# Two softmax attentions: scores from 32 bit operands in four row groups instead of three-part bf16 operands

## The reference, cut to what matters

```python
# layer 1, attn: causal self attention, 16 heads of 16 features
q, k = rope(x @ wq), rope(x @ wk)
scores = q k^T / sqrt(16);  scores = where(causal, -inf, scores)
out = softmax(scores) @ v @ wo
# layer 3, xattn: 32 heads of 8 features, keys and values from ctx (4, 256, 128)
q = axial_rope(x @ Wq, pos);  k = axial_rope(ctx @ Wk, pos);  v = ctx @ Wv
out = softmax(q k^T / sqrt(8)) @ v @ Wout + bout
```

## Time and profile before

| | |
|---|---|
| median of 3 runs | 1967.25 us (1962.34 to 1968.82) |
| profiled execution, its own time | 1948.46 us |
| its span in the trace | 1946.4 us |
| stage `l1a_` in the trace | about 538.6 to 709.5 us |
| stage `l3x_` in the trace | about 1476.4 to 1711.6 us |
| PE / DVE / ACT / POOL busy over the span | 58% / 59% / 24% / 30% |

### The profile page before, as it was taken

One profiled execution on the slowest core, in us unless ns is written; L12 is line 12 of the kernel. 1 busy time (PEld: TensorE's weight loads), 2 busy tenths in 40 slices (PEclk: granted clock), 3 DMA queues, 4 the chain that ended last, 5 costly groups with the idle time before them and its releaser, 6 DMA issues. The chain is left out here.

```text
span 1946.4 us, 22954 instructions
## 1 busy us (share of the span) xinstructions
PE 1119.3 (58%) x5620; PEld 702.2 (36%) x5620; DVE 1150.2 (59%) x2022; ACT 473.9 (24%) x881; POOL 581.0 (30%) x616
## 2 busy tenths in 40 slices
PE   4326545995063862652597802698855358837870
PEld 2202133774032640211354602576523124425650
DVE  5759965443353545998876596331346548566443
ACT  2143301221011434330211100242221226602320
POOL 0026612443620112662200063024322022204545
PEclk9669976998586886996698856799977669967995
DMA  6023318993309202331000001225310450067973
GB/s 209 1 90 139 120 65 244 309 309 97 96 0 164 34 1 90 136 123 65 1 0 1 1 11 33 79 86 147 119 33 0 114 82 3 3 206 238 271 219 102
DMA packets 146198, 196.56 MB, mean 101 GB/s; under 512 B 35056, under 2 KB 109954, under 8 KB 145484
## 3 DMA queue, kind: packets, MB, share of 16 engines
q1 hardware_dynamic: 109996, 144.47, 25.6%
q0 software_dynamic: 12608, 31.26, 5.7%
q10 hardware_dynamic: 23520, 19.93, 3.3%
HBM read 153.55 MB, written 41.75 MB: 100 GB/s over the span
## 5 line engine op out<-in xcount | busy, mean ns | idle before, releaser
L163 PE MATMUL psum<-w_ident,h 128*128 128x128 f32 x144 | 32.9, 422 | 182.5 <-DVE h L144 182.5
L1499 DVE TENSOR_REDUCE l3x_neg<-psum 128x2 f32<-128x512 f32 x128 | 80.8, 684 | 61.9 <-PE psum L1371 61.9
L453 PE MATMUL psum<-l1s_conv_out,w_ident 128*128 128x512 f32 x128 | 65.0, 632 | 83.4 <-DVE l1s_conv_out L550 83.4
L453 PE MATMUL psum<-l0s_conv_out,w_ident 128*128 128x512 f32 x128 | 65.6, 638 | 81.2 <-DVE l0s_conv_out L550 81.2
L163 PEld LDWEIGHTS psum<-w_ident,h 128*128 128x128 f32 x144 | 29.2, 224 | 185.8 <-DVE h L144 173.5
L175 ACT ACTIVATE hT<-psum 128x512 f32<-128x512 f32 x40 | 21.7, 595 | 305.1 <-PE psum L163 262.7
L1474 ACT ACTIVATE l3x_work<-psum 128x512 f32<-128x512 f32 x128 | 72.3, 600 | 77.0 <-PE psum L1393 76.7
L152 POOL TENSOR_SCALAR rstd<-moments 128x8 f32<-128x8 f32 x12 | 2.9, 240 | 282.8 <-DVE moments L140 282.8
L419 POOL TENSOR_TENSOR l0s_xpad<-l0s_du,l0s_bc 128x1024 f32<-128x1024 f32 x32 | 75.3, 2354 | 32.5 <-DVE psum L546 32.3
L419 POOL TENSOR_TENSOR l1s_xpad<-l1s_du,l1s_bc 128x1024 f32<-128x1024 f32 x32 | 75.2, 2353 | 32.5 <-DVE psum L546 32.3
L952 PE MATMUL psum<-l0f_w_in,l0f_xT 128*128 (+1 forms) x224 | 78.0, 472 | 0.0
(11 more groups left out here) (610 smaller groups left out, 3226.3 us busy)
## 6 DMA issues: line engine op xcount, KB each, us to landing
l0f_w_in<-in_l0f_w_in SPq DMA_DIRECT2D x56, 352.0 KB
l0s_bc<-l0s_scratch SPq DMA_DIRECT2D x16, 1024.0 KB, 5.2
l1s_bc<-l1s_scratch SPq DMA_DIRECT2D x16, 1024.0 KB, 5.2
l3f_w_in<-in_l3f_w_in SPq DMA_DIRECT2D x64, 192.0 KB
l0f_w_down<-in_l0f_w_down SPq DMA_DIRECT2D x56, 176.0 KB
l2f_w_in<-in_l2f_w_in SPq DMA_DIRECT2D x24, 352.0 KB
l3f_y_rows<-h SPq DMA_DIRECT2D x16, 512.0 KB, 7.1
l3f_y_rows<-l3f_y ACTq DMA_DIRECT2D x64, 128.0 KB
```

What stands on the lines that cost most here:

```text
L163: ins = nc.tensor.transpose(m.psum[:, at:at + P], m.h[:, t, k * P:(k + 1) * P], m.ident[:])
L453: ins = nc.tensor.matmul(m.pair(2 + c)[:, cols], lhsT=m.ident[:], rhs=rhs[:, cols], start=start, stop=stop, skip_group_check=True)
L1499: ins = nc.vector.tensor_reduce(self.neg[k % 2][:, :, hl], bank[:, 0:self.keys].rearrange("p (q k) -> p q k", q=self.maxima), AX_X, ALU.ma ...
```

## The change

Both attentions drop the bf16 parts.

- The rotated q and k stay fp32, and go from SBUF to SBUF: one DMA a head and a side (`load`), 16 or 8 rows of 1024 fp32, no DRAM between. Head h lies on partitions 32(h%4) and up of tile h//4. SP issues two thirds of these, ACT one third. At the stage's start SP also issues nine DMAs from DRAM: ones to partition 31 of each group of 32 in k, and zeros to the rows between the head's features and row 31 in q and k (15 rows of 16 KB in `l1a_`, 23 rows of 32 KB in `l3x_`, eight times).
- Natural matmuls contract 31 rows, turned ones 32 (with row 31 the negative maximum). The scale is applied by the exp.
- POOL no longer splits the maxima. PE transposes them as fp32, DVE copies 8 rows, SP issues two DMAs a block of eight heads.
- PE takes a pair of heads of each kind at a time in both stages: it waits for the room of both naturals and both turneds first, then issues their matmuls part by part, so that four matmuls in a row use the four row groups (`LAG` is 18). In the causal case the masks (bf16, 128 rows, unchanged in number) follow the parts that they close.
- The copies of the slots neg, out and outT come before the two maxima of a step.
- In `l3x_`, k is projected and rotated before q, the angles and the first k projection come before the transposes of h on PE, and DVE takes the angles out of PSUM while it waits for `rstd`.

```diff
-    LAG = 16
+    LAG = 18
+    GROUPS = 4
-        self.parts = [sb(tag + f"parts{i}", [P, 3, T], BF16) for i in range(2 * KD)]
-        self.packed = {x: sb(tag + f"{x}_packed", [P, self.tiles, T], BF16) for x in "qk"}
+        self.packed = {x: sb(tag + f"{x}_packed", [P, self.tiles, T]) for x in "qk"}
-    def slots_of(self, s):
+    def slots_of(self, s0):
...
+        for s in (s0, s0 + 1):
+            if s % 8 == 0 and 0 <= (s - 32) // 8 < blocks:
+                found.append(("out", (s - 32) // 8))
+            if s % 8 == 3 and 0 <= (s - 11) // 8 < blocks:
+                found.append(("neg", (s - 11) // 8))
+            if s % 8 == 5 and 0 <= (s - 37) // 8 < blocks and ((s - 37) // 8 + 1) % per_batch == 0:
+                found.append(("outT", (s - 37) // 8 // per_batch))
+        return found + [("max", s) for s in (s0, s0 + 1) if s < n]
...
+        b, h = divmod(i, self.heads)
+        return b, 32 * (h % self.GROUPS), h // self.GROUPS, h
+    def load(self, eng, i, by):
+        x, c = self.order[i]
+        eng.wait_ge(self.rot_ready, i + 1)
+        for hh in range(self.hpc):
+            if (hh % 3 == 2) == (by == "scalar"):
+                _, base, tile, _ = self.head(c * self.hpc + hh)
+                eng.dma_start(self.packed["qk"[x]][base:base + self.hd, tile, :],
+                              self.rotated[i][hh * self.hd:(hh + 1) * self.hd, :]).then_inc(self.loaded[tile], 16)
     def sync(self, sp):
+        rows = lambda name, n: self.m.dram[name].rearrange("p (h t) -> p h t", t=T)[0:n, 0:self.tiles, :]
+        sp.dma_start(self.packed["k"][31:P:32, :, :], rows("row_of_ones", self.GROUPS)).then_inc(self.filled, 16)
+        for base in range(0, P, 32):
+            for x in "qk":
+                sp.dma_start(self.packed[x][base + self.hd:base + 31, :, :], rows("zeros", 31 - self.hd)).then_inc(self.filled, 16)
+        for i in range(2 * KD):
+            self.load(sp, i, "sync")
+        for k in range(self.n // self.BLOCK):
+            b, _, tile, _ = self.head(k * self.BLOCK)
+            sp.wait_ge(self.turn_emptied, self.slot("neg", k) + 1)
+            for u in range(self.BLOCK // self.GROUPS):
+                sp.dma_start(self.packed["q"][31:P:32, tile + u, b * S:(b + 1) * S],
+                             self.neg_rows[k % 2][u * self.GROUPS:(u + 1) * self.GROUPS, :]).then_inc(self.neg_loaded[k % 2], 16)
...
+        pe.wait_ge(self.filled, 16 * (1 + 2 * self.GROUPS))
...
+            for i in naturals:
+                natural_room(i)
+            for i in turneds:
+                turned_room(i)
+            for part in range(3 if self.causal else 2):
+                kt = part if not self.causal else (0, None, 1)[part]
+                for i in naturals:
+                    natural(i, part)
+                if kt is not None:
+                    for i in turneds:
+                        turned(i, kt)
+                if self.causal and kt is not None:
+                    for i in naturals:
+                        natural_mask(i, part)
+                    for i in turneds:
+                        turned_mask(i, kt)
+            if s0 % 4 == 0 and 0 <= (s0 - 24) // 4 < n // self.QUAD:
+                mix((s0 - 24) // 4)
...
-            for i, scale in enumerate(scales):
-                a.split_scalar(act, i, scale)
+            for i in range(2 * KD):
+                a.load(act, i, "scalar")
```

More of the change, by code:

```diff
@@ L1188, in __init__ @@
         self.n = B * heads
[L1189 to L1192, removed]
+        self.order = [(x, c) for c in range(KD) for x in ((0, 1) if causal else (1, 0))]
+        self.tiles = heads // self.GROUPS
         self.stride = self.hd + 1
@@ L1220, in __init__ @@
          self.whole_ready) = (
[L1221 to L1226, removed]
@@ L1232, in slots_of @@
+    def slots_of(self, s0):
         n, blocks = self.n, self.n // self.BLOCK
+        per_batch = self.heads // self.BLOCK
         found = []
[L1234 to L1242, removed]
@@ L1402, in turned @@
-            ins.then_inc(self.scored, 1)
+        def turned(i, kt):
+            out, q, k = self.bank(3 + i % 3), rows("q", i, 1), rows("k", i, 1)
+            first = kt * P if self.causal else 0
+            ins = nc.tensor.matmul(out[:, kt * S:(kt + 1) * S - first], lhsT=k[:, kt * P:(kt + 1) * P], rhs=q[:, first:],
+                                   start=True, stop=not self.causal, skip_group_check=True)
+            if kt == 1 and not self.causal:
+                ins.then_inc(self.scored, 1)
@@ L1446, in features @@
             ins.then_inc(self.turn_filled, 1)
-        pe.wait_ge(self.ident_ready, 2 if self.causal else 1)
+        if self.causal:
+            pe.wait_ge(self.ident_ready, 2)
         pe.wait_ge(self.v_ready, 2)
-        make = {"max": natural, "neg": negative, "out": back, "outT": features}
+        pe.wait_ge(self.filled, 16 * (1 + 2 * self.GROUPS))
         last = n // self.BLOCK - 1
-        for s0 in range(0, n + 40, step):
-            for s in range(s0, s0 + step):
-                for kind, i in self.slots_of(s):
-                    if (kind, i) == ("out", last):
+        for s0 in range(0, n + 40, 2):
+            for kind, i in self.slots_of(s0):
+                if kind == "out":
+                    if i == last:
@@ L1456, in tensor @@
                         before_last()
-                    make[kind](i)
-            for s in range(s0, s0 + step):
-                if 0 <= s - self.LAG < n:
-                    turned(s - self.LAG)
-            for s in range(s0, s0 + step):
-                if s % 4 == 2 and 0 <= (s - 22) // 4 < n // self.QUAD:
-                    mix((s - 22) // 4)
-    def scalar(self, act):
+                    back(i)
+                elif kind == "neg":
+                    negative(i)
+                elif kind == "outT":
+                    features(i)
@@ L2270, in decoder @@
                          for tag in ("l0f_", "l2f_", "l3f_")}
-        m.neg_sems = {tag: [m.sem(tag + f"neg_loaded{i}") for i in range(2)] for tag in ("l1a_", "l3x_")}
         stored = m.sem("stored")
```

270 lines of the change are left out of this document (94 added, 176 removed).

## The result

The changed kernel takes **2195.57 us** (median of 4 runs, 2188.86 to 2196.82); the kernel before took 1968.03 beside it (1962.34 to 1973.09). The ratio is 1.117, 95% interval 1.112 to 1.122. I had forecast 1956 us: the sign is wrong, and the time lies far outside the range. The profiled execution has a span of 2187.0 us, 240.6 more than before.

The account below looks back on a forecast made before the run. PE was taken to bound `l1a_`, DVE and its hand-overs with PE `l3x_`. Terms of -1.5 us (`l1a_`) and -10 (`l3x_`) sum to -11.5: 1967.25 - 11.5 = 1956 us, range 1905 to 1992 (the forecast's own 1940 to 1972).

Parts of the forecast that it names:

- Zeros of `l3x_`: On SP's queue before the loads: 8 x 736 KB at 200 KB/us, 30 us, done by 1507.
- The rival beside it: Zeros hold up the loads of `l3x_`: start 1542, +21, time 1977; chance 0.13.
- Starts without the zeros: Loop starts: `l1a_` at 590.3 instead of 612.8, `l3x_` at 1521 instead of 1552.2.
- The stretches with two row groups: Loop ends, naturals or turneds alone: nine steps each, at 1.86 and 1.9 in `l3x_`, 2.06 and 2.07 in `l1a_`.
- +4 for the clock: First steps of the `l3x_` loop at half speed after PE idles nearly 4 us: +4.
- The steady pace: Eight heads in the steady loops: 9.15 in `l3x_` (9.3 with outT), 11.5 in `l1a_` (11.8 with outT).
- The wait for a whole pair: PE waits for DVE's first reduce before the next pair: 1.86 in `l3x_`; for the second after a slot: 2.46.
- Row groups side by side in fp32: Score matmuls on four row groups overlap as the mix does on columns: a pair in `l3x_` costs 0.92.
- the dear rival: fp32 row groups (L1307, L1332) do not run side by side: 2013 if only neighbours overlap, 2115 if none; chance 0.08 for both.
- Waits for rows of maxima: PE's waits for these DMAs in the loops, five times, 22.4 us in `l3x_` before: none after the change.

Follow-up runs that it names:

- the banks: Changed kernel with zeros as 16 and 7 rows, and four PSUM banks instead of three in the naturals' ring: ratio 1.030 to the kernel before.
- four banks and the earlier copy: Changed `l3x_` with memset zeros, four banks, ACT's copy of a mix a step earlier, `l1a_` as before: ratio 0.994 to the kernel before.
- three kernels: `l1a_` with all masks (pace 11.94), with none (7.88, ratio 0.999), with turned masks alone (11.04, ratio 1.019); the last two on the memset version.

## Why the prediction was wrong

By its own steps, against the stage starts (the start of `l1a_` is 3.3 us later after the change, that of `l3x_` 26.3, of which `l1a_` makes 20.7):

- **Zeros of `l3x_`: the step that failed.** The sum took the 5.9 MB at the 200 KB/us of a 1 MB load, 30 us, done by 1507 and so at no cost to the start. The rival beside it says: "At half that rate (23 rows do not divide over 16 engines) they end at 1537, and the loop starts at about 1542". Its place and its reason were right, the size was not: one engine of 16, 27 GB/s, and neither 200 nor 100. The eight DMAs take 223 us. The start came 232.6 us after the stage instead of 44.6: 188 of the miss. I had halved a rate where the row count said that the engines might not share the rows at all. The other bound stood in the earlier trace rows: 200 GB/s over 16 engines is 12.5 for one, 470 us for 5.9 MB. The time measured lies between, and a range that kept it would have been wide.
- **Starts without the zeros**: right and a little cautious (37.8 against 44.6; `l1a_` at 588.5 against 590.3). No rotation or v copy was late.
- **The stretches with two row groups: mis-sized.** I had nine steps at 1.86 and +4 for the clock in `l3x_`, and nothing for it in `l1a_`. Measured for the naturals alone: 27.3 us (21 forecast) and 28.5 (18.5), both at PEclk 0.50 to 0.55. The turneds alone at the end take 22 us (17) and 28 (18.6), at 0.84 and 0.70, and the part between is some 6 and 8 us longer, with its first turned blocks at half clock. The loops take 184 and 132 us instead of 166 and 105: 18 and 27 of the miss.
- **The steady pace**: nearly right (9.37 against 9.15 and 11.94 against 11.5 without outT), from a sum of steps that came out within 0.25 us each. The wait for a whole pair was right, but is one of three that stand at the same place, as the banks showed.
- **Row groups side by side in fp32**: right; the dear rival did not come.
- **Waits for rows of maxima**: gone, as said.

The terms add up: 188 + 18 + 27, less 5 for the earlier start of `l1a_` (46.6 after its stage, 51.7 forecast), is 228, and the forecast -11.5 becomes +216.5; the two stages measure +216.6.

With the zeros' DMAs cured alone the change is still slower (1.02 to 1.04). What it lacked beyond that shows in the runs: the masks between the row groups, the clock at its ends, and the two waits that four banks and the earlier copy take away.

## What to carry to other kernels

Look at the number of rows of each DMA before its bytes: eight DMAs of 23 rows went over one engine each and cost 188 us, eight of 32 rows went at 194 GB/s. When a step is priced by pairs, write down every wait that ends at its start; taking the named one away shows only the next. And where rows are padded with zeros for a matmul, ask what the clock does without them before removing them.

## What the runs showed of the hardware that I had not expected

- The granted clock followed the rows that the matmuls contract. In the steady loop of `l1a_`: 31 and 32 rows in four groups 1.00, 23 and 24 rows 0.50 for two blocks and then 0.90 to 1.00, 16 and 17 rows 0.50 up to the last block; in `l3x_` 1.00, 1.00, and 0.57 with 8 and 9 rows. With the naturals of two row groups it was 0.50 even while added matmuls of all rows kept PE busy for all of 29.80 us. Two row groups alone do not decide it either: at the end of `l3x_`, where only turneds, mixes and transposes run, the same instructions had 0.61 in one trace (16 and 7 rows of zeros, 28.4 us) and 0.84 to 1.00 in the others with 31 and 32 rows (22.4 us or less). How these follow from one rule, no run here settles.
- With mask matmuls between the fp32 ones the clock was lower at `l1a_`'s end: 0.58 to 0.70 in the eight traces with all of them and 31 and 32 rows, 1.00 in both without.
- Two memsets on POOL stopped DVE's scalings for their whole length: 15.94 us for eight that take 2.67.
- fp32 matmuls on four row groups started within 0.04 us of one another, and a group's next entry 0.22 us later.
- A change of tiling cost 0.10 us by the starts in one pair of `l1a_`; the 0.14 by the difference of three kernels holds lost overlap as well.
